# Cross attention of a decoder layer: scores of a late and an early tile made together, in four rows of 32x32 tiles

## The chip, the core and the metric

The kernel runs on one NeuronCore of a Trainium2 chip. The metric is the device time of one execution in microseconds (us). A core has engines that run side by side, each with its own queue of instructions in program order: TensorE (PE in the rows; its weight loads are PEld), VectorE (DVE), ScalarE (ACT), GpSimd (POOL) and SyncE (SP), which issues the transfers here. They wait for each other by semaphores. TensorE writes into PSUM, 8 banks of 128 partitions by 512 fp32 columns.

## What is computed

One post-norm decoder layer over 128 sequences of 64 tokens, 128 features, all in fp32: linear attention with 16 heads, a feed-forward layer with a table lookup, cross attention, and a small mixture of experts. The change touches the cross attention and the last lines of the mixture's gate. Cut to them:

```python
def _L0_xattn_ref(x, encoder_output, mask, WQ, WK, WV, WO):      # H = 16 heads of 8
    q = (x @ WQ)...; k = (encoder_output @ WK)...; v = (encoder_output @ WV)...
    scores = jnp.einsum('bhqd,bhkd->bhqk', q, k) / SQRT_DK
    future = jnp.triu(jnp.ones((s, s), jnp.int32), 1)
    m = mask[:, None, :, None] + future[None, None, :, :]
    scores = jnp.where(m != 0, NEG, scores)
    attn = jax.nn.softmax(scores, axis=-1)
    ctx = jnp.einsum('bhqk,bhkd->bqhd', attn, v).reshape(b, s, d)
    return ctx @ WO
```

The gate is a softmax over 7 experts, of which the two largest weights are kept, divided by their sum, and used on one expert's output.

## The kernel before

The 8192 tokens are 64 tiles of 128, in 16 groups of four. Three phases run over the groups one after the other: linear attention (phase 1), feed-forward (phase 2) and, from about 250 us on, cross attention and mixture (`phase3` of each engine, called with step s). In step s of phase 3 the attention of group s is done, the projections of group s+1 are prepared, the attention output of group s-1 is projected, added and normalised and its experts are multiplied, and the mixture of group s-2 is finished. Each step has four slots, t = 0 to 3, one for each tile n = 4s + t. The order of the work is written out by hand: each engine's `phase3` lists, slot by slot, what it does, and runs it in that order.

**Late and early tiles.** A tile holds 32 queries of four sequences. An even n is a late tile (queries 32 to 63, over all 64 keys), an odd n an early one (queries 0 to 31, over the 32 keys that they may see). Late scores take all 512 columns of the two banks of `pair[0]`, early scores 256 columns of the two banks of `pair[1]`.

**Scores.** TensorE's array is used in 32x32 tiles. A quad is four heads: 32 rows of features of `qT` (so one row of tiles of the array), and a matmul of quad and sequence gives 32 queries by 4 heads of keys. `k_exp` holds the keys of each of the four heads apart, zero elsewhere, so that one matmul gives all four. `scores_open(n)` writes the causal mask as the start of the sum (L1228, bf16, 8 matmuls in rows 0 and 2 of the array) and adds quads 0 and 2 (L1210, 8 matmuls, each of which runs as two passes and so has two records); `scores_close(n)` adds quads 1 and 3 (L1210). Quads 0 and 1 go into one bank, 2 and 3 into the other, so the two of one bank are in different calls.

**From scores to output.** DVE `shift(n)` takes the largest score of each head (L930) and subtracts it (L936 early; L943 late, in two halves); ACT `probabilities(n)` takes the exponential (L718); PE `turn_probabilities` transposes it back into the score banks (L1242), late 8 transposes, early 4; ACT `copy_pT` copies it out (L725); PE `weigh_values` multiplies by the values into bank 7 (L1270 late, L1254 and L1261 early); DVE `xattend` divides (L918, L920). Since the turned probabilities use the score banks, `scores_open(n+2)` waits for `copy_pT(n)`.

**The rest of a step.** PE: `turn_y` (L1051, X), K and Q projections (L1279), V projection (L1290), attention transposes (L1342) and output projection (L1325), transposes of the normalised rows (L1051, xn), experts (L1298). DVE: residual add (L1011) and statistics (L290, L297) in slot 1, `gate_top` (L952 to L957) and `future_keys` (L1000) in slot 0, `gate_weights` (seven operations, each waiting for the one before, L972 to L982) in slot 2, `mixture` (L988 and statistics) in slot 3. POOL: `spread_k` (L514, makes `k_exp`), bias (L537), normalisation of group s-1 (L305 to L327, into `y2`), `spread_v` (L526), normalisation of group s-2 (the same lines).

## Time and profile before

| | |
|---|---|
| Median of 3 runs | 574.67 us (572.77, 574.67 and one of 655.31) |
| The profiled execution | 573.05 us, its span 571.3 us |
| TensorE busy | 514.6 us, 90% of the span |
| VectorE busy | 425.5 us, 74% |
| ScalarE busy | 358.6 us, 63% |
| GpSimd busy | 347.7 us, 61% |
| Chain that ended last | TensorE 74%, ScalarE 9%, VectorE 7%, issue 7% |

Busy shares are averages over the phases. In the rows a time like 399.08 is microseconds from the start of the span; the second number of a timeline row is how long its instructions were busy; the next row of the same engine can begin before that has passed, since instructions of an engine overlap, so the distance from start to start is what one costs its engine. What stands in square brackets is idle time just before, and who ended it.

### The profile page before, as it was taken

The numbers are of one execution on the slowest core, as the hardware profiler recorded it, in microseconds if no ns is written. First come the engines' busy times: TensorE is split into PE (matmuls) and PEld (weight loads), VectorE is DVE, ScalarE is ACT, GpSimd is POOL, SyncE is SP. The second block draws the span as 40 slices with busy tenths as digits, with TensorE's granted clock in tenths as the row PEclk, the third lists the DMA queues.
The fourth block names the chain that finished last, engine by engine and source line by source line (L and its number), as shares of the span: only waits on it lengthen the run. The fifth ranks groups of instructions, "written<-read, shape, count | busy, mean of one in ns | idle before, by whom it ended". The sixth has DMA issues, their size and how long they took to land.

```text
span 571.3 us, 23478 instructions
## 1 busy us (share of the span) xinstructions
PE 514.6 (90%) x9568; PEld 371.0 (65%) x9568; DVE 425.5 (74%) x1468; ACT 358.6 (63%) x643; POOL 347.7 (61%) x666
## 2 busy tenths in 40 slices
PE   2899999989999999988999999999999999999740
PEld 1677777767777777665666666666666666666530
DVE  2777777656777666565778898889888898889743
ACT  1565656657777778748657765677657666677320
POOL 6666666644577766631556666765776657765463
PEclk9999999999999999999999999999999999999775
DMA  6630000000000000011001011110111011100001
GB/s 165 178 100 2 3 2 3 2 3 1 1 2 1 2 1 2 1 40 27 26 3 48 5 49 50 49 27 26 49 50 47 7 49 49 50 22 3 23 18 37
DMA packets 24731, 17.47 MB, mean 31 GB/s; under 512 B 2096, under 2 KB 22448, under 8 KB 24624
## 3 DMA queue, kind: packets, MB, share of 16 engines
q1 hardware_dynamic: 24192, 15.90, 9.8%
q8 instruction: 76, 1.25, 0.9%
q14 instruction: 31, 0.25, 0.2%
q10 hardware_dynamic: 432, 0.07, 0.1%
HBM read 11.77 MB, written 4.19 MB: 28 GB/s over the span
## 4 chain that ended last, share of the span: by engine, by line
PE 74%; ACT 9%; DVE 7%; issue 7%; POOL 3%; DMA 1%; DVEq 0%; POOLq 0%; ACTq 0%
PE pair L1196 10%; PE pair L1160 9%; PE pair L1056 8%; PE pair L1242 7%; PE pair L1210 6%; PE pair L1051 6%; PE pair L1279 4%; PE pair L1270 3%; PE pair L1128 3%; ACT v L706 3%; PE pair L1298 3%; PE pair L1290 2%; PE pair L1228 2%; PE pair L1325 2%; ACT gel L718 2%
## 5 line engine op out<-in xcount | busy, mean ns | idle before, releaser
L725 ACT ACTIVATE gel<-pair 128x1024 f32<-128x1024 f32 x64 | 51.9, 810 | 63.0 <-PE pair L1242 63.0
L718 ACT ACTIVATE gel<-gel,row_scale 128x512 f32<-128x512 f32 x96 | 66.1, 720 | 33.1 <-DVE gel L943 20.7
L1210 PE MATMUL pair<-k_exp,qT 32*32 32x128 f32 (+1 forms) x2048 | 68.5, 327 | 0.2 <-PE pair L1210 0.2
L1196 PEld LDWEIGHTS pair<-w,gel 128*128 128x128 f32 x512 | 60.4, 192 | 8.0 <-issue 5.7
L1196 PE MATMUL pair<-w,gel 128*128 128x128 f32 x512 | 62.5, 276 | 1.0 <-ACT gel L651 1.0
L930 DVE TENSOR_REDUCE neg_max<-pair 128x16 f32<-128x1024 f32 x64 | 60.8, 950 | 1.6 <-PE pair L1210 1.3
L1160 PE MATMUL pair<-hT,w 128*128 128x512 f32 x128 | 58.2, 595 | 1.3 <-ACT lev L646 1.3
L1242 PE MATMUL pair<-ident,gel 128*128 128x128 f32 x384 | 56.1, 282 | 2.4 <-ACT gel L718 2.4
L526 POOL COPY v<-v 32x256 f32<-32x256 f32 x64 | 26.6, 416 | 51.3 <-ACT v L706 48.3
L1242 PEld LDWEIGHTS pair<-ident,gel 128*128 128x128 f32 x384 | 42.2, 141 | 21.1 <-issue 15.3
L514 POOL TENSOR_SCALAR k_exp<-k_sb,quad_mask 128x512 f32<-128x512 f32 x64 | 43.0, 687 | 6.0 <-issue 3.6
L1051 PE MATMUL pair<-ident,xn 128*128 128x128 f32 x192 | 31.5, 289 | 16.1 <-POOL xn L327 16.1
L1298 PE MATMUL pair<-w_moe,y2T 128*128 128x263 f32 x128 | 39.7, 440 | 6.7 <-ACT moe_out L732 6.0
L305 POOL TENSOR_SCALAR veps_b<-mv_b 128x4 f32<-128x4 f32 x32 | 7.7, 242 | 62.4 <-DVE mv_b L297 32.0
L943 DVE TENSOR_TENSOR gel<-pair,neg_max 128x512 f32<-128x512 f32 x64 | 41.2, 686 | 1.1
L491 POOL TENSOR_TENSOR X<-X,proj_sb 128x512 f32<-128x512 f32 x16 | 20.3, 1272 | 35.6 <-ACT proj_sb L609 35.6
L1051 PEld LDWEIGHTS pair<-ident,xn 128*128 128x128 f32 x192 | 23.4, 147 | 28.1 <-issue 17.0
L1160 PEld LDWEIGHTS pair<-hT,w 128*128 128x128 f32 x128 | 22.9, 190 | 23.8 <-issue 23.5
L651 ACT ACTIVATE gel<-lev 128x512 f32<-128x512 int8 x64 | 36.3, 619 | 0.1
L307 POOL TENSOR_TENSOR rstd_b<-veps_b,minus_half 128x4 f32<-128x4 f32 x32 | 34.1, 1065 | 2.7
L290 DVE BATCH_NORM_STATS2 stats<-X 128x6 f32<-128x128 f32 x128 | 27.6, 278 | 10.2 <-DMA X<-in_x 10.2
L307 POOL TENSOR_TENSOR rstd<-veps,minus_half 128x4 f32<-128x4 f32 x32 | 33.2, 1038 | 2.7
(127 smaller groups left out, 1231.4 us busy)
## 6 DMA issues: line engine op xcount, KB each, us to landing
X<-in_x SPq DMA_DIRECT2D x16, 256.0 KB, 3.0
cT<-in_ctx SPq DMA_DIRECT2D x16, 256.0 KB, 3.8
out_rows<-X SPq DMA_DIRECT2D x16, 256.0 KB, 2.5
mask_rows<-in_mask_early SPq DMA_DIRECT2D x16, 128.0 KB, 3.8
w<-in_L_attn_w SPq DMA_DIRECT2D x2, 256.0 KB, 3.4
w_kv<-in_L_attn_wk SPq DMA_DIRECT2D x1, 64.0 KB, 3.0
w_q<-in_L_attn_wq ACTq DMA_DIRECT2D x1, 64.0 KB, 2.6
w_kv<-in_L_attn_wv SPq DMA_DIRECT2D x1, 64.0 KB, 2.9
```

The source lines that it names most:

```text
L307: nc.gpsimd.tensor_tensor(rstd[:, :], veps[:, :], minus_half[:, :], ALU.pow)\
L514: last = nc.gpsimd.tensor_scalar(k_exp[q][:, h, :], k_sb[:, :], quad_mask[:, h:h + 1], 0.0, ALU.mult, ALU.add)
L718: nc.scalar.activation(part, part, ACT.Exp, scale=row_scale[:, n:n + 1])\
L725: nc.scalar.activation(pT[par], flat[:, 0:GW] if n % 2 else flat, ACT.Copy)\
L930: nc.vector.tensor_reduce(neg_max[par][:, :].rearrange("p (a h) -> p a h", a=2), scores, AX.X, ALU.max, negate=True).then_inc(max_ready, 1)
L1051: last = nc.tensor.transpose(dst[:, P * t:P * (t + 1)], src[:, t, :], ident[:, :])
L1056: last = nc.tensor.matmul(dst[:, P * t:P * (t + 1)], src[:, P * t:P * (t + 1)], w, start=True, stop=True)
L1160: nc.tensor.matmul(bank(up_bank(s, f)), w_1[:, P * f:P * (f + 1)], hT[p][:, :], start=True, stop=True).then_inc(up_done, 1)
L1196: last = nc.tensor.matmul(bank(6 + q)[:, P * t:P * (t + 1)], gel[:, q, f, P * t:P * (t + 1)], w_2[:, f, :], start=(f == 0), stop=(f == NF ...
L1210: last = nc.tensor.matmul(pair[t % 2][b * QW:(b + 1) * QW, quad // 2, heads], qT[p][rows, batch + first:batch + first + QW], k_exp[p][rows ...
L1242: last = nc.tensor.transpose(flat[:, P * i:P * (i + 1)], probability_rows(n)[:, P * i:P * (i + 1)], ident[:, :])
L1298: nc.tensor.matmul(bank(MOE_BANK[t])[:, 0:2 * D + NE], y2T[:, P * t:P * (t + 1)], w_moe[:, :], start=True, stop=True).then_inc(moe_done, 1)
```

## The change

TensorE makes the scores of late tile n+2 and early tile n+3 in one `scores_open` and one `scores_close`, both in the even slots. The late tile opens with quads 0 and 2 and the early one with quads 1 and 3; they close the other way round. So each call has all four rows of the array, going to four different banks. The early tile's mask is written from rows 1 and 3; for that the mask's constants are filled for all four blocks of 32 partitions (four selects of 32 partitions in place of two of 64, in phase 2 on POOL). The early tile's turned probabilities go into columns 256 to 511 of their banks, so its next scores need not wait for their copy, but for its `shift` (`sub_ready`). VectorE's `shift` of an even tile waits until both closes are done, and of an odd one also for the copy of the early probabilities before, since both use one bank.

The order in `phase3` is written anew on PE, DVE and ACT. POOL's and SP's is as before. `gate_weights` takes six operations in place of seven: `top_sum` is the product of the sum and its reciprocal.

```diff
@@ ACT @@
-                flat = pair[par][:, :, :].rearrange("p a c -> p (a c)")
-                nc.scalar.activation(pT[par], flat[:, 0:GW] if n % 2 else flat, ACT.Copy)\
+                turned = pair[par][:, :, HH * QW:] if n % 2 else pair[par][:, :, :]
+                nc.scalar.activation(pT[par].rearrange("p (a c) -> p a c", a=2), turned, ACT.Copy)\
                     .then_inc(pT_ready, 1)
...
@@ DVE @@
             def shift(n, par):
 
-                dve.wait_ge(s_done, n + 1)
+                dve.wait_ge(s_done, n + 2 if n > 0 and n % 2 == 0 else n + 1)
+                if n % 2:
+                    after(dve, pT_ready, n - 1)
...
-                chain(nc.vector.tensor_tensor(top_w[:, :, :], top_p[:, :, :],
-                                              top_s[:, :].unsqueeze(2).broadcast_to([P, TG, 2]),
-                                              ALU.mult))
-                chain(nc.vector.tensor_reduce(top_sum[:, :], top_w[:, :, :], AX.X, ALU.add))
+                chain(nc.vector.tensor_tensor(top_sum[:, :], top_z[:, :], top_s[:, :], ALU.mult))
...
@@ PE @@
+            def scores_open(*ns):
+
+                n = ns[0]
+                after(pe, pT_ready, n - 1)
+                if n > 1:
+                    pe.wait_ge(sub_ready, shifted(n - 1, 0))
+                if n % TG == 0:
+                    pe.wait_ge(kexp_ready, n // TG + 1)
+                    pe.wait_ge(q_ready, n // TG + 1)
+                for n in ns:
+                    future_scores(n)
+                for n in ns:
+                    quad_scores(n, (1, 3) if n % 2 else (0, 2)).then_inc(s_opened, 1)
+
+            def scores_close(*ns):
+
+                pe.wait_ge(s_opened, ns[-1] + 1)
+                for n in ns:
+                    quad_scores(n, (0, 2) if n % 2 else (1, 3)).then_inc(s_done, 1)
...
+                    if exists(s) and t % 2 == 0 and n + 2 < NT:
+                        scores_open(n + 2, n + 3)
                     if exists(s):
                         if t == 0:
                             pe.wait_ge(v2_ready, s + 1)
-                        if s == 0 and t == 0:
+                        if n == 0:
                             pe.wait_ge(ysum_ready, NG)
-                        if s * TG + t + 2 < NT:
-                            scores_open(s * TG + t + 2)
-                        weigh_values(s * TG + t, t, p)
+                        weigh_values(n, t, p)
+                    if exists(s) and t % 2 == 0 and n + 2 < NT:
+                        scores_close(n + 2, n + 3)
```

On TensorE, slots 2 and 3 of a step in the middle of phase 3 stand before like this (`k_exp,qT` are quads, `causal_bf` the mask, `ident,gel` the turned probabilities, `v,gel` the weighing, `ident,xn` the transposes into bank 6):

```order
L1242 MATMUL pair<-ident,gel 128x128 x8
L1290 MATMUL pair<-w_xv,cT 64x64 x16
L1228 MATMUL pair<-causal_bf,ident_bf 32x512 x8
L1210 MATMUL pair<-k_exp,qT 32x256 x8
L1270 MATMUL pair<-v,gel 32x18 x32
L1210 MATMUL pair<-k_exp,qT 32x256 x8
L1242 MATMUL pair<-ident,gel 128x128 x4
L1051 MATMUL pair<-ident,xn 128x128 x4
L1228 MATMUL pair<-causal_bf,ident_bf 32x256 x8
L1210 MATMUL pair<-k_exp,qT 32x128 x8
L1254 MATMUL pair<-v,future 32x144 x4
L1261 MATMUL pair<-v,gel 32x36 x16
```

The same slots of the changed kernel:

```order
L1267 MATMUL pair<-ident,gel 128x128 x8
L1315 MATMUL pair<-w_xv,cT 64x64 x16
L1236 MATMUL pair<-causal_bf,ident_bf 32x512 x8
L1236 MATMUL pair<-causal_bf,ident_bf 32x256 x8
L1221 MATMUL pair<-k_exp,qT 32x256 x8
L1221 MATMUL pair<-k_exp,qT 32x128 x8
L1295 MATMUL pair<-v,gel 32x18 x32
L1221 MATMUL pair<-k_exp,qT 32x256 x8
L1221 MATMUL pair<-k_exp,qT 32x128 x8
L1267 MATMUL pair<-ident,gel 128x128 x4
L1062 MATMUL pair<-ident,xn 128x128 x4
L1279 MATMUL pair<-v,future 32x144 x4
```

The early tile's mask and quads have moved out of slot 3 and stand directly behind the late tile's in slot 2; slot 3 has no scores left.

On VectorE, from the `xattend` of slot 1 to the start of `gate_weights`, with the semaphores waited for, before:

```order
L918 RECIPROCAL rec<-pair 128x16 [waits pv_done]
L920 TENSOR_TENSOR att<-pair,rec 128x128 [waits xrec_ready]
L930 TENSOR_REDUCE neg_max<-pair 128x16 [waits s_done]
L936 TENSOR_TENSOR gel<-pair,neg_max 128x512 [waits p_xposed,max_ready]
L972 TENSOR_REDUCE top_z<-top_e 128x4 [waits tope_ready]
```

The same stretch of the changed kernel:

```order
L931 TENSOR_REDUCE neg_max<-pair 128x16 [waits pT_ready,s_done]
L937 TENSOR_TENSOR gel<-pair,neg_max 128x512 [waits p_xposed,max_ready]
L917 RECIPROCAL rec<-pair 128x16 [waits pv_done]
L919 TENSOR_TENSOR att<-pair,rec 128x128 [waits xrec_ready]
L973 TENSOR_REDUCE top_z<-top_e 128x4 [waits tope_ready]
```

The early `shift` now stands ahead of the `xattend` of slot 1. In the whole step VectorE's order is now: `gate_top`, `future_keys`, `xattend` (slot 0); late `shift`, residual add and statistics, early `shift`, `xattend`, `gate_weights` (slot 1); `xattend` (slot 2); late `shift`, `xattend`, early `shift`, `mixture` (slot 3). Before, each slot began with one `shift`, and `xattend` ended it.

## Rows read from the trace of the kernel before

**Rows 1.** Windows: busy time by engine, granted clock, DMA share; phase 2, a light, a full step
```profile
150.00:200.00 50.00, 50.00 (x291) 36.61 (x291) 35.35 (x153) 37.31 (x73) 36.17 (x74) 1.00 0.01 1
...
269.00:287.20 18.20, 17.65 (x459) 12.25 (x457) 12.11 (x33) 12.23 (x21) 7.49 (x15) 1.00 0.09 26
397.25:415.51 18.26, 17.71 (x459) 12.18 (x458) 16.25 (x55) 12.39 (x22) 12.10 (x23) 1.00 0.14 39
```

**Rows 2.** Timeline, TensorE, one full step: start, busy, line, operands, count
```profile
391.56 0.66 PE L1051 MATMUL pair<-ident,xn 128*128 128x128 f32 x4
...
395.83 0.71 PE L1298 MATMUL pair<-w_moe,y2T 128*128 128x263 f32 x2 [0.44 <-ACT moe_out L732]
...
399.08 0.41 PE L1228 MATMUL pair<-causal_bf,ident_bf 32*32 32x512 bf16 x8
399.31 0.61 PE L1210 MATMUL pair<-k_exp,qT 32*32 32x256 f32 x16
399.85 0.74 PE L1270 MATMUL pair<-v,gel 128*32 128x18 f32 x64
400.52 0.66 PE L1210 MATMUL pair<-k_exp,qT 32*32 32x256 f32 x16
401.12 0.66 PE L1242 MATMUL pair<-ident,gel 128*128 128x128 f32 x4
...
403.45 0.30 PE L1228 MATMUL pair<-causal_bf,ident_bf 32*32 32x256 bf16 x8
403.57 0.40 PE L1210 MATMUL pair<-k_exp,qT 32*32 32x128 f32 x16
403.90 0.45 PE L1254 MATMUL pair<-v,future 128*32 128x144 f32 x8
...
404.59 0.45 PE L1210 MATMUL pair<-k_exp,qT 32*32 32x128 f32 x16
404.96 1.09 PE L1242 MATMUL pair<-ident,gel 128*128 128x128 f32 x8
```

**Rows 3.** Timeline, VectorE, the same step
```profile
399.08 0.36 DVE L952 MAX8 top<-moe_out 128x8 f32<-128x8 f32 x4
...
400.72 0.26 DVE L918 RECIPROCAL rec<-pair 128x16 f32<-128x16 f32 x1 [0.57 <-PE pair L1270]
...
401.29 1.22 DVE L930 TENSOR_REDUCE neg_max<-pair 128x16 f32<-128x1024 f32 x1
402.55 1.29 DVE L943 TENSOR_TENSOR gel<-pair,neg_max 128x512 f32<-128x512 f32 x2
403.76 0.68 DVE L1011 TENSOR_TENSOR X<-X,pair 128x512 f32<-128x512 f32 x1
...
406.03 0.22 DVE L918 RECIPROCAL rec<-pair 128x16 f32<-128x16 f32 x1
...
406.50 0.68 DVE L930 TENSOR_REDUCE neg_max<-pair 128x16 f32<-128x512 f32 x1
...
407.82 0.18 DVE L972 TENSOR_REDUCE top_z<-top_e 128x4 f32<-128x32 f32 x1
...
409.12 0.16 DVE L982 TENSOR_REDUCE top_sum<-top_w 128x4 f32<-128x8 f32 x1
409.31 0.26 DVE L918 RECIPROCAL rec<-pair 128x16 f32<-128x16 f32 x1
...
412.27 1.69 DVE L988 SCALAR_TENSOR_TENSOR moe_out<-moe_out,top_sum 128x128 f32<-128x128 f32 x4
...
415.55 0.23 DVE L918 RECIPROCAL rec<-pair 128x16 f32<-128x16 f32 x1
```

**Rows 4.** Timeline, POOL, a later full step
```profile
507.78 0.23 POOL L305 TENSOR_SCALAR veps_c<-mv_c 128x4 f32<-128x4 f32 x1 [1.15 <-DVE mv_c L297]
...
511.33 2.69 POOL L514 TENSOR_SCALAR k_exp<-k_sb,quad_mask 128x512 f32<-128x512 f32 x4
513.99 1.29 POOL L537 TENSOR_TENSOR moe_out<-moe_out,bias_bc 128x512 f32<-128x512 f32 x1
516.63 0.24 POOL L305 TENSOR_SCALAR veps_b<-mv_b 128x4 f32<-128x4 f32 x1 [1.35 <-issue]
```

More of the change, by code:

```diff
@@ L443, in late_constants @@
                 if part in (1, 2):
-                    b = part - 1
-                    c = causal[b * S:(b + 1) * S, :, :]
-                    const(select(out=c, in_=c, compare_op=ALU.is_ge, fill=NEG, base=S - QW,
-                                 pattern=[[0, HH], [-1, S]], channel_multiplier=1))
+                    for b in (2 * part - 2, 2 * part - 1):
+                        c = causal[b * QW:(b + 1) * QW, :, :]
+                        const(select(out=c, in_=c, compare_op=ALU.is_ge, fill=NEG, base=S - QW,
+                                     pattern=[[0, HH], [-1, S]], channel_multiplier=1))
                 if part in (3, 4):
@@ L754, in phase3 @@
                         nc.scalar.activation(attT[:, :], bank(6), ACT.Copy).then_inc(xattT_ready, 1)
+                    if t == 0 and exists(nxt):
+                        copy_y(nxt)
                     if t == TG - 1 and exists(prev):
@@ L1006, in phase3 @@
                 for t in slots:
-                    if exists(s) if t < TG - 1 else exists(s + 1):
-                        shift(s * TG + t + 1, (t + 1) % 2)
+                    n = s * TG + t
+                    if n == 0:
+                        shift(1, 1)
+                    if t == 0 and exists(old):
+                        dve.wait_ge(moe_ready, (s - 1) * TG)
+                        gate_top(old, p)
+                    if t == 0 and exists(s + 1):
+                        future_keys(s + 1, q)
+                    if t == 0 and exists(s):
+                        after(dve, xatt_xposed, s - 1)
+                        xattend(n, p, t)
+                    if t == 1 and exists(s):
+                        shift(n + 1, 0)
                     if t == 1 and exists(prev):
@@ L1016, in phase3 @@
                                       stats_b, mv_b, ln_b.done, prev)
+                    if t == 1 and exists(s):
+                        shift(n + 2, 1)
+                        xattend(n, p, t)
+                    if t == 1 and exists(old):
+                        gate_weights(old)
+                    if t == 2 and exists(s):
+                        xattend(n, p, t)
+                    if t == 3 and exists(s + 1):
+                        shift(n + 1, 0)
+                    if t == 3 and exists(s):
+                        xattend(n, p, t)
+                    if t == 3 and exists(s + 1) and s >= 0:
+                        shift(n + 2, 1)
                     if t == 3 and exists(old):
                         mixture(old, p)
-                    if t == 0 and exists(old):
-                        dve.wait_ge(moe_ready, (s - 1) * TG)
-                        gate_top(old, p)
-                    if t == 0 and exists(s + 1):
-                        future_keys(s + 1, q)
-                    if t == 2 and exists(old):
-                        gate_weights(old)
-                    if exists(s):
-                        if t == 0:
-                            after(dve, xatt_xposed, s - 1)
-                        xattend(s * TG + t, p, t)
             pipeline(dve, phase1, last=NG - 1)
@@ L1213, in quad_scores, with future_scores @@
                             k_exp[p][rows, :, batch:batch + width],
-                            start=False, stop=quad % 2 == 1)
+                            start=False, stop=quad % 2 != n % 2)
                 return last
-            def scores_open(n):
-                after(pe, pT_ready, n - 1)
-                if n % TG == 0:
-                    pe.wait_ge(kexp_ready, n // TG + 1)
-                    pe.wait_ge(q_ready, n // TG + 1)
+            def future_scores(n):
                 width = QW if n % 2 else S
                 for half in range(2):
-                    rows = slice(half * FH, half * FH + QW)
+                    quad = 2 * half + n % 2
+                    rows = slice(quad * QW, (quad + 1) * QW)
                     future = causal_bf[rows, :].rearrange("p (h k) -> p h k", k=S)[:, :, S - width:]
@@ L1344, in phase3 @@
                         last.then_inc(xatt_xposed, 1)
+                    if t == 0 and exists(g):
+                        after(pe, moe_ready, (s - 1) * TG - 1)
+                        after(pe, v2_ready, g)
+                        turn_y(g)
+                    if t == 1 and exists(r):
+                        pe.wait_ge(xattT_ready, r + 1)
+                        rows_product(bank(6), attT, w_xo[:, :]).then_inc(xproj_done, 1)
                     if t == 1 and exists(g):
@@ L1347, in phase3 @@
                         project_qk(yT, w_xq, bank(4), xq_done)
+                    if t == 2 and exists(g):
+                        pe.wait_ge(q_ready, g + 1)
+                        project_v(g, q)
+                    if t == 3 and exists(r):
+                        pe.wait_ge(ln_b.done, r + 1)
+                        transposes(y2, bank(6), y2_xposed)
+                    if exists(s) and t % 2 == 0 and n + 2 < NT:
+                        scores_open(n + 2, n + 3)
                     if exists(s):
```

82 lines of the change are left out of this document (30 added, 52 removed).

## The prediction

> **What bounds the kernel now.** I read the windows first, then the timelines of the engines over one step. The change touches phase 3 only, so the question is what sets the length of one step there. In the windows [rows 1] a full step takes 18.26 us, with TensorE busy for 17.71 and VectorE for 16.25; the granted clock is 1.00, the higher of the two levels (2.4 GHz). A light step, of the first two, has no mixture yet: 18.20 us, TensorE 17.65, VectorE only 12.11. So TensorE sets the light steps. In a full step TensorE's timeline shows one wait, 0.44 us ahead of the expert matmul that needs its bank copied out [rows 2]: 18.26 - 0.44 = 17.82 us of work. VectorE's busy sum leaves out what lies between dependent operations on itself; its timeline has one real wait, 0.57 us for the weighing in slot 0 [rows 3], so its own work takes 18.26 - 0.57 = 17.69 us. Two engines are full within 0.6 us of each other. Whatever TensorE saves in a full step, VectorE gives back only up to 0.57 us of it. That is the core of this forecast.
>
> **What the change saves on TensorE.** From start to start [rows 2]: the late tile's mask and quads 0 and 2 take 399.85 - 399.08 = 0.77 us (0.23 and 0.54), its closing quads 401.12 - 400.52 = 0.60. The early tile's take 403.90 - 403.45 = 0.45 (0.12 and 0.33) and 404.96 - 404.59 = 0.37. A pair costs 2.19 us. If the early tile's matmuls run in the two rows of the array that the late tile leaves free, a pair costs what the late tile costs, 1.37 us, and up to 0.05 more for the starts of another 24 matmuls. Do they run together? Before, two rows by four columns do: 8 matmuls of 256 columns in 0.54 us and of 128 columns in 0.33, so the time goes with the columns of one and hardly with the count. Four rows by four columns are not in the trace. Bounds: from below 1.37, nothing added; from above 2.19 for rows that do not overlap. I take 1.42, because the weighing, a 128-row form that reads all four row blocks at once for four column tiles, starts 64 passes in 400.52 - 399.85 = 0.67 us, about 10 ns each, and nothing there is slower for using all rows. TensorE saves 2 x (2.19 - 1.42) = 1.5 us a step: 17.82 becomes 16.3.
>
> The Trainium skill, TensorEngine Tiling (Array Packing), Instruction Overhead, puts some 60 cycles of overhead on each matmul. By it the 80 starts of a pair (16 masks, 64 passes of quads) would cost about 2.0 us at 2.4 GHz, an estimate from that page, whether they share the array or not, and the change would save next to nothing. The trace disagrees: passes start 10 ns apart in the weighing.
>
> **What VectorE has left.** The gate loses one operation; from the last one's start to the next instruction is 409.31 - 409.12 = 0.19 us [rows 3]. I take 0.2. Its work becomes 17.49 us. All its other operations are only reordered. So a full step can't be shorter than 17.49, and the question is what waits the new order leaves.
>
> Pieces from start to start [rows 3]: `gate_top` and `future_keys` 400.72 - 0.57 - 399.08 = 1.07; `xattend` 406.50 - 406.03 = 0.47 (0.5 below); late `shift` 403.76 - 401.29 = 2.47; add and statistics 406.03 - 403.76 = 2.27; early `shift` 407.82 - 406.50 = 1.32; gate 409.31 - 407.82 - 0.2 = 1.29; mixture 415.55 - 412.27 = 3.28. A signal from one engine to another takes about 0.13 us behind the end shown (weighing ends at 399.85 + 0.74 = 400.59, VectorE starts at 400.72).
>
> Wait one: slot 2. `scores_open(n+2, n+3)` waits for the early `shift` just done. Then TensorE needs 0.13 + 0.79 (open) + 0.67 (weigh) + 0.63 (close) + 0.13 = 2.35 us until the late `shift` may start. VectorE meanwhile does `xattend`, gate, `xattend`: 0.5 + 1.29 + 0.5 = 2.29. It waits 0.1 us. In slot 0 the same loop is covered by mixture, `gate_top` and `future_keys`, over 4.3 us.
>
> Wait two: slot 3. K is now projected at the end of slot 0 and copied in slot 1, so POOL's `spread_k` starts later, and POOL's pieces close up into one chain behind the mixture's statistics [rows 4]: normalise group s-2 511.33 - 507.78 = 3.55, spread 2.66, bias 1.29, normalise group s-1 3.45 (the same operations as the 3.55), 10.9 us. With 0.3 for the signal ahead (their wait of 1.15 ended that long after the statistics), then 0.13, transposes 0.66, weighing 404.59 - 403.90 = 0.69, 0.13, the `xattend` of slot 3 is free 12.8 us after the mixture. VectorE gets there after 1.07 + 0.5 + 2.47 + 2.27 + 1.32 + 0.5 + 1.29 + 0.5 + 2.47 = 12.4. It waits 0.4, or 0.3 if it has already waited 0.1. TensorE's wait for the same transposes, near 0.8 us, falls into its 1.2 us of slack.
>
> The added waits of the early `shift` (copy of the probabilities before) and of the late one (both closes) cost nothing: the copy lies some 3 us earlier, behind the turn in slot 1, and the early close ends with the late one. Without that cover a `shift` would hold up everything behind it on VectorE. The expert matmul's 0.44 us wait on TensorE goes too, since the turn now stands ahead of it. The two extra selects on POOL lie in phase 2, where TensorE is busy for 50.00 of 50 us and POOL for 36 [rows 1]; nothing.
>
> **The sum.** Full step: 17.49 + 0.1 + 0.3 = 17.9 us against 18.26, 0.35 saved; some twelve of them, 4.2. Light steps: the one in the rows, and the next, whose mixture comes only at its end, so that VectorE goes through it with the room of the one before. TensorE 18.20 - 1.5 = 16.7, 1.5 saved each, 3.0. The first fill, the last two steps and the emptying, where engines wait for each other in a chain, I leave as they are. 573.05 - 7.2 = 565.9, say **566 us**, against a profiled execution of 573.05; that lies within 2 us of the two close runs of before (572.77 and 574.67).
>
> The page's rule on the PSUM Bottleneck (TensorEngine Tiling (Array Packing), the Trainium skill) says that tiling speeds up TensorE but not the reading of PSUM. The trace agrees: 0.57 us of room on VectorE against 1.5 saved.
>
> **Rivals.**
> - *The waits don't appear.* If POOL's chain or the loop in slot 2 is 0.4 us shorter than I make it, a full step falls to 17.49: 12 x 0.77 + 3.0 = 12.2, 560.8 us. For it: both waits are small differences of long sums. Against it: both sums are on the edge at once. 16%.
> - *Scores overlap in part.* With 0.15 us more in both open and close, wait one becomes 0.4, and the full steps save 0.1 to 0.2: 1.8, the light ones 1.8: 569.5. With the waits a bit longer, up to 573. 14%.
> - *The other side: the four rows don't overlap.* A pair costs 2.19 as before, open 1.22 and close 0.97. Then in slot 2 TensorE needs 0.13 + 1.22 + 0.67 + 0.97 + 0.13 = 3.12 us against VectorE's 2.29: it waits 0.83, and a full step takes 17.49 + 0.83 + 0.3 = 18.6: 12 x 0.36 = 4.3 us lost, 577 us. It decides from about 0.3 us more in each call. For it: the form is not in the trace. Against it: two rows do overlap, into two banks, and here are four banks. 7%.
> - *Starts bind, as by the page.* Then 2.0 us a pair, near 576. 2%.
> - *A wait that I don't see* holds VectorE for 1 us a step (the V copy, moved to slot 2, or the early order of the copies on ScalarE, 12.4 us busy of 18.3): 585. 3%.
>
> The forecast itself, 563 to 569.5, has the other 58%.
>
> **The numbers.** From 560 to 573 holds the forecast, nearly all of the first rival and the second. About 2%, 11.5 us, is what a measurement of this kernel can tell from no change: faster than 561.5 is two thirds of the first rival and a little of the forecast's edge, 14%; slower than 584.5, 3%; the rest within.
>
> **What would show it.** Right: in the changed profile a close of late and early quads takes about 0.6 us from start to start, and an open 0.8; the full step is 17.9 us, with VectorE idle for 0.1 us for the quads and 0.3 for the early weighing and TensorE idle for 1.2 us or more, ahead of the masks (for the early `shift`) and of the `xn` transposes (for POOL); POOL without a pause from L305 of group s-2 to L327 of group s-1. Wrong: quads of 0.9 us, a step above 18.2, or VectorE waiting for a semaphore of ScalarE.

## The result, and the profile after

| | before | changed |
|---|---|---|
| Median | 572.7 us (20 runs) | 575.63 us (20 runs, from 571.04) |
| Ratio to before | 1 | 1.0043, 95% interval 1.0027 to 1.0059 |
| Profiled execution, its span | 573.05, 571.3 us | 575.97, 574.2 us |
| TensorE busy | 514.6 us, 90% | 498.4 us, 87% |
| VectorE busy | 425.5 us, 74% | 415.1 us, 72% |

The change takes 16 us of busy time off TensorE and 10 off VectorE, and the kernel is 0.4% slower: its interval lies above 1, though well inside the 2% that the prediction counts as no change. 566 was forecast, with a range from 560 to 573. One run of each kernel, of 655.31 and of 2618.49 us, stands far above its others and hardly moves a median of 20.

First the timeline of TensorE over one step of the changed kernel in which little is disturbed (one stop of 0.20 us, at 410.78; start, busy, line, operands, count; idle time before in brackets). It answers to [rows 2].

```profile
399.86 0.60 PE L1062 MATMUL pair<-ident,X 128*128 128x128 f32 x4
400.39 0.41 PE L1236 MATMUL pair<-causal_bf,ident_bf 32*32 32x512 bf16 x16
400.61 0.70 PE L1221 MATMUL pair<-k_exp,qT 32*32 32x256 f32 x32
401.24 0.78 PE L1295 MATMUL pair<-v,gel 128*32 128x18 f32 x64
401.95 0.66 PE L1221 MATMUL pair<-k_exp,qT 32*32 32x256 f32 x32
402.54 1.13 PE L1304 MATMUL pair<-cT,w_xk 128*128 128x512 f32 x2
...
409.11 0.41 PE L1236 MATMUL pair<-causal_bf,ident_bf 32*32 32x512 bf16 x16 [0.47 <-ACT gel L724]
...
412.50 0.66 PE L1062 MATMUL pair<-ident,xn 128*128 128x128 f32 x4 [0.18 <-POOL xn L326]
...
417.03 0.60 PE L1062 MATMUL pair<-ident,X 128*128 128x128 f32 x4
```

An open takes 401.24 - 400.39 = 0.85 us and a close 0.59: a pair 1.44. The step takes 17.17 us against 18.26. So the saving is there. But most steps don't look like this. In TensorE's waits from 250 to 545 us (line, what was waited for, us in total, times, longest) the changed kernel has these two entries:

```profile
PE pair L1221 <- issue: 10.7, 9, 2.1
PE pair L1295 <- issue: 2.1, 3, 1.3
```

In the kernel before, the same view has these:

```profile
PE pair L1261 <- issue: 0.6, 1, 0.6
PE pair L1270 <- issue: 0.5, 1, 0.5
```

"Issue" is time in which an engine waited for nothing that the profile shows. Here is one such place, on TensorE's timeline:

```profile
463.06 0.71 PE L1221 MATMUL pair<-k_exp,qT 32*32 32x256 f32 x32
463.70 0.77 PE L1295 MATMUL pair<-v,gel 128*32 128x18 f32 x64
464.40 0.61 PE L1221 MATMUL pair<-k_exp,qT 32*32 32x256 f32 x2
467.09 1.10 PE L1221 MATMUL pair<-k_exp,qT 32*32 32x256 f32 x30 [2.08 <-issue]
```

Two passes of a closing quad run, then the engine stands still for 2.1 us in the middle of one call, which has no wait inside it, and then the other 30 run. VectorE waits for these quads. Its busiest groups on the page answer for that: first of the changed kernel,

```profile
L931 DVE TENSOR_REDUCE neg_max<-pair 128x16 f32<-128x1024 f32 x64 | 60.6, 946 | 16.2 <-PE pair L1221 15.6
```

where before the idle time ahead of that operation was 1.6 us.

**Where the time went.** TensorE's transposes of X mark the steps of phase 3. Before:

```profile
251.95 0.60 PE L1051 MATMUL pair<-ident,X 128*128 128x128 f32 x4
268.89 0.60 PE L1051 MATMUL pair<-ident,X 128*128 128x128 f32 x4
287.09 0.60 PE L1051 MATMUL pair<-ident,X 128*128 128x128 f32 x4
507.59 0.60 PE L1051 MATMUL pair<-ident,X 128*128 128x128 f32 x4
```

and changed:

```profile
253.11 0.60 PE L1062 MATMUL pair<-ident,X 128*128 128x128 f32 x4
271.02 0.60 PE L1062 MATMUL pair<-ident,X 128*128 128x128 f32 x4
292.84 0.60 PE L1062 MATMUL pair<-ident,X 128*128 128x128 f32 x4
508.83 0.60 PE L1062 MATMUL pair<-ident,X 128*128 128x128 f32 x4
```

The last row is twelve steps behind the third. From the differences of these rows, with the kernel of the experiment e4 (below; its four rows start at 253.06, 271.21, 288.65 and 500.65, its span is 562.4) beside them:

| us | before | changed | forecast of the difference | difference | e4, difference to before |
|---|---|---|---|---|---|
| up to the first | 251.95 | 253.11 | 0 | +1.2 | +1.1 |
| two light steps | 35.14 | 39.73 | -3.0 | +4.6 | +0.5 |
| twelve full steps | 220.50 | 215.99 | -4.2 | -4.5 | -8.5 |
| the rest | 63.7 | 65.4 | 0 | +1.7 | -2.0 |
| span | 571.3 | 574.2 | -7.2 | +2.9 | -8.9 |

The full steps come out as forecast, but by two errors that cancel, as will be seen; the rest of the miss lies in the light steps and at the ends.

### The profile page after: what moved, and what is told of

Same layout as the page of the kernel before. It is cut to its first block, busy times and chain, and to the rows that moved or that the text cites. A ratio compares the mean times of both kernels' runs of the same rounds, so it can differ in the third digit from the quotient of the medians.

```text
span 574.2 us, 23512 instructions
## 1 busy us (share of the span) xinstructions
PE 498.4 (87%) x9568; PEld 376.2 (66%) x9568; DVE 415.1 (72%) x1452; ACT 356.5 (62%) x643; POOL 346.8 (60%) x668
## 3 DMA queue, kind: packets, MB, share of 16 engines
q8 instruction: 76, 1.25, 0.9%
## 4 chain that ended last, share of the span: by engine, by line
PE 69%; DVE 12%; POOL 7%; issue 7%; ACT 2%; DMA 1%; DVEq 0%; POOLq 0%; ACTq 0%
PE pair L1067 9%; PE pair L1207 9%; PE pair L1171 9%; PE pair L1221 6%; PE pair L1062 6%; PE pair L1267 5%; PE pair L1323 5%; PE pair L1304 4%; DVE neg_max L931 3%; PE pair L1139 3%; PE pair L1295 3%; POOL k_exp L513 2%; DVE gel L944 2%; PE pair L1081 2%; PE pair L1097 2%
## 5 line engine op out<-in xcount | busy, mean ns | idle before, releaser
L1221 PE MATMUL pair<-k_exp,qT 32*32 32x128 f32 (+1 forms) x2048 | 49.4, 332 | 10.8 <-issue 10.7
L1267 PEld LDWEIGHTS pair<-ident,gel 128*128 128x128 f32 x384 | 44.1, 143 | 21.0 <-issue 15.3
L304 POOL TENSOR_SCALAR veps_c<-mv_c 128x4 f32<-128x4 f32 x16 | 3.9, 246 | 84.1 <-DVE mv_c L296 73.2
L1062 PE MATMUL pair<-ident,xn 128*128 128x128 f32 x192 | 32.1, 294 | 19.6 <-POOL xn L326 19.4
L1221 PEld LDWEIGHTS pair<-k_exp,qT 32*32 32x32 f32 x2048 | 26.1, 103 | 16.7 <-issue 13.5
```

Source lines behind the costliest of these rows:

```text
L1062: last = nc.tensor.transpose(dst[:, P * t:P * (t + 1)], src[:, t, :], ident[:, :])
L1221: last = nc.tensor.matmul(pair[t % 2][b * QW:(b + 1) * QW, quad // 2, heads], qT[p][rows, batch + first:batch + first + QW], k_exp[p][rows ...
L1267: last = nc.tensor.transpose(dst, probability_rows(n)[:, P * i:P * (i + 1)], ident[:, :])
```

## The theory

**Supply.** All long "issue" gaps inside a group of like matmuls fall at one place of TensorE's instruction count. With all of its records in the trace (weight loads, matmul passes and its semaphore instructions) numbered by their start, from 0, the first record behind such a gap has the remainder 193 on division by 256, in every kernel of this study. That record is called the border of a block below. TensorE's instructions come in by transfers of their own: on the page the queue

```profile
q8 instruction: 76, 1.25, 0.9%
```

moves 76 packets of 1.25 MB in all, 16 KB each, and TensorE has 19489 records, 76.1 times 256. In e4, with 18721 records (73.1 times 256), it moves 73 packets. So instructions arrive in blocks of 256. The theory: when TensorE uses up a block faster than the next can be had, it stands still at the border. A block of the new dense stretch (open, weighing, close: some 290 records in 2.2 us, where before it was some 200 with slower work on both sides) is used up in as little as 1.8 us. From the records, time to use up a block, from 252 to 545 us. A gap is given here, and in the table of the experiments, from the start of the record before it to the start of the one behind: 2.45 us for the stop of 2.08 above.

| | before | changed |
|---|---|---|
| blocks used up in under 2.9 us; followed by a gap over 0.3 us; gaps | 1; 0; none | 8; 8; 0.9 to 2.5 us |
| in 2.9 to 4 us | 18; 2; up to 0.8 | 13; 4; up to 1.4 |
| in over 4 us | 37; 1; 0.4 | 35; 0; none |

The gaps at borders inside masks, quads and weighing sum to 2.0 us in 3 places before, and 16.7 in 12 after; of that, TensorE is idle for 1.1 and 12.8 us. The number of instructions is not the reason: a full step has 924 records before and 925 after. The new order only sets them closer.

**The transfers themselves.** The trace has the time of each of the 76 packets, and they settle the theory. Four stops of the changed kernel, in us:

| TensorE begins a block | packet of the next block starts | has landed | TensorE begins the next block | after landing |
|---|---|---|---|---|
| 282.04 | 283.80 | 284.68 | 286.09 | 1.41 |
| 417.57 | 417.56 | 418.91 | 420.31 | 1.40 |
| 461.81 | 464.64 | 465.59 | 467.09 | 1.50 |
| 519.29 | 520.40 | 521.65 | 523.10 | 1.45 |

All 12 gaps of the changed kernel end 1.2 to 1.5 us after a packet has landed, the two over 0.5 us of the kernel before 1.4 us after, and those of e3 (below) 1.2 to 1.6. In none of the traces of this study does any block begin sooner than 1.19 us after its packet has landed. So a packet's transfer starts about when TensorE begins the block before it (in the changed kernel from 0.9 us ahead to 2.8 behind, 1.1 behind in the median), takes about 1.0 us, and its instructions can run some 1.4 us later. An estimate from these three: a block that is used up in less than their sum, 3.5 us in the usual case, ends in a stop. The sum varies; in the 12 gaps it was from 2.7 to 5.3 us.

**The stops cost a second time, by the clock.** The granted clock of TensorE falls to the lower of its two levels (1.2 GHz) behind three of the longer stops of the changed kernel (1.85, 2.08 and 1.62 us), at about 286, 467 and 525 us. Windows around the second (busy time of PE, PEld, DVE, ACT, POOL, then the granted clock), and TensorE's timeline there:

```profile
463.00:467.00 4.00, 2.01 (x114) 1.26 (x99) 1.72 (x9) 1.65 (x3) 3.70 (x8) 1.00 0.21 52
467.00:471.00 4.00, 3.91 (x79) 2.69 (x78) 2.51 (x3) 1.47 (x3) 0.83 (x2) 0.57 0.01 4
```

```profile
468.12 1.11 PE L1267 MATMUL pair<-ident,gel 128*128 128x128 f32 x4
469.03 1.06 PE L1062 MATMUL pair<-ident,xn 128*128 128x128 f32 x4
470.02 0.68 PE L1279 MATMUL pair<-v,future 128*32 128x144 f32 x8
```

The transposes of the normalised rows take 470.02 - 469.03 = 0.99 us from start to start, against 0.59 in the step shown first (412.50 to 413.09). The stretch from 467.09 to 470.94 costs TensorE some 1.4 us more than the same work there, so the three cost about 4 us, an estimate. In the kernel before, and in e4, the clock stays at 1.00 from 252 to 525 us. The second step of phase 3 shows both prices: 21.8 us against e4's 17.4, of which two stops are 0.92 + 1.85 and the clock some 1.4. Stops of 0.62 and 1.62 us and the third stretch lie behind 508.83, in "the rest" of the table above, which is 1.7 us longer than before.

The rival: the gaps are hidden semaphore waits, or the four rows of the array disturb each other, or the new order has a wait that the trace doesn't name.

## The experiments

All on the changed kernel except where a base is named. The ratio is to the kernel before, with its 95% interval. "Gaps" are those at block borders inside masks, quads or weighing over the whole kernel, from about 0.14 us up, in us (from start to start, as above) and places.

| | us | ratio | records per step | gaps |
|---|---|---|---|---|
| e1 same rows | 582.4 | 1.0186 (1.0129, 1.0243) | 925 | 12.3 in 11 |
| e2 border beside the dense stretch | 572.6 | 0.9993 (0.9972, 1.0014) | 1023 | 14.1 in 19 |
| e3 border in the dense stretch | 601.3 | 1.0494 (1.0453, 1.0535) | 1023 | 38.5 in 28 |
| e4 few masks | 566.0 | 0.9891 (0.9829, 0.9954) | 877 | 3.9 in 5 |
| e11 the same again | 567.4 | 0.9905 (0.9874, 0.9936) | 877 | 5.6 in 5 |
| e5 before, few masks | 578.6 | 1.0094 (1.0070, 1.0118) | 876 | 0.9 in 3 |
| e6 few masks, same rows | 574.9 | 1.0035 (1.0012, 1.0059) | 877 | 4.8 in 7 |
| e7 before, gate of six | 571.6 | 0.9977 (0.9965, 0.9990) | 924 | 1.9 in 4 |
| e8 borders moved once | 572.2 | 0.9972 (0.9940, 1.0005) | 925 | 8.5 in 9 |
| e9 slot 0 spread | 583.9 | 1.0197 (1.0179, 1.0216) | 925 | 14.4 in 12 |
| e10 few masks, slot 0 spread | 579.9 | 1.0125 (1.0094, 1.0157) | 877 | 5.8 in 7 |

**e2 and e3: moving the borders.** Tiny matmuls (32x32x32, bf16, two records each) fill a step up to four blocks, so that the borders stay at the same work in every step. The two kernels differ in one number: where e2, shown here, has `fillers(50, 5)` once ahead of the first step, e3 has `fillers(114, 5)`, 128 records more.

```diff
+            def fillers(count, dst):
+                for i in range(count):
+                    r = slice(i % QB * QW, (i % QB + 1) * QW)
+                    nc.tensor.matmul(bank(dst)[r, 0:32], ident_bf[r, r], causal_bf[r, 0:32],
+                                     start=True, stop=True)
...
                         scores_close(1)
+                        fillers(50, 5)
...
+                    if t == 2 and s > 0 and exists(g):
+                        pe.wait_ge(k_ready, g + 1)
+                        fillers(12, 5)
+                    if t == 3 and s > 0 and exists(g):
+                        fillers(37, 5)
```

> The changed kernel with small extra matmuls (2 instructions each, into a free bank, results unused): 12 in slot 2 and 37 in slot 3 of steps 1 to 14, where TensorE waits anyway, so that a step has about 1024 instructions, four blocks of 256; and 50 once ahead of the first step, so that a block's border falls in the middle of each dense stretch (open, weigh, close: 290 instructions in 2.1 us). Theory S: the gaps inside quads and weighing nearly vanish (under 2 us of 12.8) and the time is 562 to 568 us, though there is more to do. Theory R, or any theory in which the blocks don't matter: gaps as before, 575 us or a little more.

> The same as the kernel with the split blocks, but 114 extra matmuls ahead of the first step in place of 50, so that in every step a whole block lies inside a dense stretch. Theory S: a gap of 1 to 2.5 us at the end of nearly every dense stretch, some 28 of them, 30 to 50 us in all, of which each step's slack takes 1 to 2 us: 585 to 610 us. Theory R or no effect of blocks: the same time as the one with the split blocks plus the 0.6 us of the 64 further matmuls.

e3 is 28.7 us slower than e2, for 64 tiny matmuls once, of which 37 run in 0.36 us. TensorE's waits of e3:

```profile
PE pair L1221 <- issue: 26.9, 24, 1.9
```

and its timeline:

```profile
401.01 0.42 PE L1221 MATMUL pair<-k_exp,qT 32*32 32x128 f32 x8 [1.18 <-issue]
...
408.94 0.66 PE L1221 MATMUL pair<-k_exp,qT 32*32 32x256 f32 x24
410.73 0.42 PE L1221 MATMUL pair<-k_exp,qT 32*32 32x128 f32 x8 [1.13 <-issue]
411.08 1.76 PE L1304 MATMUL pair<-cT,w_xk 128*128 128x512 f32 x2
```

The stop is seven or eight passes before the end of a close, in slot 0 and slot 2 of step after step. No semaphore and no row of the array knows of this place; only the instruction count does. 27 blocks are used up in under 2.9 us, and 26 of them are followed by a gap over 0.3 us. e2 missed its expectation (562 to 568 us, gaps under 2): blocks that hold half of a dense stretch each are used up in 2.8 to 3.9 us, and most of these still end in gaps, mostly of 0.4 to 1 us, 14 us in all.

**e8: the borders moved once, no filling.** 64 tiny matmuls ahead of the first step.

```diff
                         scores_close(1)
+                        fillers(64, 5)
```

> The changed kernel with 64 tiny matmuls (128 instructions) once ahead of the first step of phase 3, nothing else: the borders of the 256-instruction blocks move by half a block against the work of every step, and a step still has 925 instructions. Supply theory: the gaps stay at the same place of TensorE's instruction count (remainder 193 of 256) but move to other lines and steps; since 925 instructions shift the border by 157 instructions in each step, the sum over sixteen steps stays about the same: 12 to 20 us of gaps, 572 to 579 us. The steps that were long (the second at 21.8 and the twelfth at 20.5 us) become ordinary and others become long. Rival (the long steps are waits of the schedule itself, in those steps): the same steps stay long.

The second and the twelfth step, 21.8 and 20.5 us long in the changed kernel, take 17.2 and 17.7; now the first (21.4) and the sixth (20.5) are long. The gaps of the table sum to 8.5 us; three more stand at borders outside that count (1.07 and 0.82 in projections and transposes, and one of 1.55 between a weighing and its close), 11.9 together, just under the 12 to 20 expected. The last of them is in the long first step:

```profile
258.91 1.11 PE L1221 MATMUL pair<-k_exp,qT 32*32 32x256 f32 x32 [1.34 <-issue]
```

There the granted clock is also at its lower level, from 255.6 to 262.4 us, behind a wait of 1.73 for VectorE that the changed kernel has too without losing the clock. So not all of that step is supply. But the second, sixth and twelfth step become ordinary or long as the count is moved, which rules out a wait of the schedule in those steps.

**e4, e5, e11: fewer instructions.** Four mask matmuls of 32x32 become one of 32x128, which writes the same bank.

```diff
-                    for b in range(QB):
-                        nc.tensor.matmul(pair[n % 2][b * QW:(b + 1) * QW, half, 0:HH * width],
-                                         ident_bf[rows, rows], future, start=True, stop=False)
+                    nc.tensor.matmul(pair[n % 2][:, half, 0:HH * width],
+                                     ident_rep[rows, :, :].rearrange("p b q -> p (b q)"),
+                                     future, start=True, stop=False)
```

> The changed kernel with the causal mask written by one matmul of 32 rows by 128 columns for each bank, in place of four of 32 by 32: 24 instructions fewer in each dense stretch (266 in place of 290), 48 fewer in a step. Theory S: the fraction of blocks that lie inside a dense stretch falls to near nothing but blocks of 2 to 3 us remain, so the gaps shrink by a third to a half: 569 to 574 us. Theory R: no change from the changed kernel, 575 us, or slower by the switches between tile forms (28 of 0.1 us).

> The kernel before, with only the few masks of e4_few_masks: each bank's mask written by one matmul of 32 rows by 128 columns in place of four of 32 by 32. It is the control for e4: how much of e4's gain has nothing to do with the pairing. A step has 877 instructions on TensorE here too. Supply theory (TensorE starves where a block of 256 instructions is used up in under about 3 us): before has few such gaps (1.96 us over phase 3), and the mask costs TensorE the same columns, so little is to be gained: 571 to 574 us, same as before. Rival (the few masks are a gain of their own, and e4 says nothing about the pairing): TensorE's share of a mask falls, 566 to 568 us.

> The kernel of e4_few_masks once more, in five rounds, for the interval: it had 565.99 us, ratio 1.1 per cent below before from four runs. Supply theory: 565 to 568 us again, ratio 0.987 to 0.992; clean steps 17.3 to 17.7 us. If its time depends on how the gaps fall from run to run, single runs spread over more than the 4 us of before.

The same edit makes the changed kernel 8 to 10 us faster and the kernel before 6 us slower. e5's timeline says why it costs something:

```profile
402.00 0.39 PE L1232 MATMUL pair<-causal_bf,ident_rep 32*128 32x512 bf16 x2
402.32 0.66 PE L1215 MATMUL pair<-k_exp,qT 32*32 32x256 f32 x16
402.91 0.74 PE L1275 MATMUL pair<-v,gel 128*32 128x18 f32 x64
```

Mask and quads take 0.91 us (0.32 and 0.59) where they took 0.77 (0.23 and 0.54) [rows 2]; the early tile's take 0.14 more too, and a step 18.55. Neither of the two cases given for e5 held: both had left out that the wide mask costs TensorE time. That makes the gain in e4 the clearer. It comes in spite of dearer masks, with the dense stretch 24 records shorter and the gaps down from 16.7 us to 3.9 and 5.6. e4 is faster than both kernels, and 3 us below its own expectation; no stretch of it between 252 and 525 us has the lower clock, which that expectation had not counted. That its 566.0 us is the figure forecast for the change is luck: other terms make it up, as shown below. e11 lands in its range; its single runs spread from 563.5 to 569.7 us, and its profiled one has the lower clock in one stretch, from 355 us.

**e1, e6: are four rows worth anything?** Both tiles' quads run in the same rows of the array again, in e1 on the changed kernel, in e6 on e4.

```diff
-                    quad = 2 * half + n % 2
-                    rows = slice(quad * QW, (quad + 1) * QW)
+                    rows = slice(half * FH, half * FH + QW)
-                    quad_scores(n, (1, 3) if n % 2 else (0, 2)).then_inc(s_opened, 1)
+                    quad_scores(n, (0, 2)).then_inc(s_opened, 1)
```

> The changed kernel, but the early tile's mask and quads use the same rows of the array as the late tile's in each call (mask and quads 0 and 2 open, 1 and 3 close), so the order is that of the changed kernel and the rows no longer overlap. Theory S (instruction supply: TensorE's instructions come in blocks of 256, and a block that is used up in under about 3 us leaves TensorE waiting for the next): a pair's open, weigh and close take about 2.9 us in place of 2.1, so the blocks last longer, the waits put down to issue inside quads and weighing fall from 12.8 us to under 5, but the loop in slot 2 costs VectorE 0.8 us a step; 575 to 579 us. Theory R (the four rows themselves disturb each other and make the gaps): no gaps, and the time falls below 572.

> e4_few_masks with the late and the early tile in the same rows of the array again (both open with quads 0 and 2): what the four rows are worth once most of the supply gaps are gone. The trace of e1 shows about 0.25 us more in an open and 0.2 in a close than the changed kernel. Supply theory with the prediction's own VectorE arithmetic: slot 2's loop grows by 0.45 us and VectorE waits that much longer once a step, light steps lose 0.9 each: 5 to 8 us more than e4, 571 to 574 us. Rival (the rows are worth nothing here, the order of the work alone gives the time): 566 to 568 us.

e1's timeline, an open, the weighing and a close:

```profile
402.22 0.52 PE L1235 MATMUL pair<-causal_bf,ident_bf 32*32 32x512 bf16 x16
402.56 0.83 PE L1221 MATMUL pair<-k_exp,qT 32*32 32x256 f32 x32
403.32 0.74 PE L1294 MATMUL pair<-v,gel 128*32 128x18 f32 x64
403.99 0.88 PE L1221 MATMUL pair<-k_exp,qT 32*32 32x256 f32 x32
404.80 1.12 PE L1303 MATMUL pair<-cT,w_xk 128*128 128x512 f32 x2
```

A pair takes 1.10 + 0.81 = 1.91 us against 1.44: four rows save 0.47 a pair, 0.94 a step. By the medians that is 6.8 us on the changed kernel and 8.9 on e4, where 5 to 8 were expected of e4. Of the 0.75 that a pair saves against before (2.19 to 1.44), 0.28 comes from issuing both tiles together and 0.47 from the rows. The forecast of few gaps for e1 was wrong: its dense stretch is only 0.4 us longer, and 12.3 us of gaps stay, so that its 582.4 us lies above the 575 to 579. With the rows apart and the gaps still there, the four rows aren't their cause.

**e7: the gate alone**, on the kernel before: six operations for seven.

> The kernel before with only the gate in six operations in place of seven. VectorE saves 0.19 us a step. The prediction took VectorE's own work for 17.69 of 18.26 us in before, TensorE sets the step with 17.82 of work plus its one wait of 0.44. Theory: the 0.19 lies on VectorE alone, and part of it reaches the step: 571 to 573 us (0 to 2 us faster). Rival (VectorE sets the full step already): the whole 0.19 in twelve to fourteen steps, 2.5 us faster, 570.3 us or less. Slower than 574 would speak against both.

1.3 us faster by the medians, with full steps of 18.27 as before. TensorE sets them, and VectorE's 0.2 us is not seen in them; where the 1.3 us comes from is not shown.

**e9, e10: spreading slot 0.** The transposes of attention output and X go between open and weighing, to thin out the dense stretch of slot 0 (in e10 on e4); shown for X, the other block moves with it.

```diff
-                    if t == 0 and exists(g):
-                        after(pe, moe_ready, (s - 1) * TG - 1)
-                        after(pe, v2_ready, g)
-                        turn_y(g)
...
                         scores_open(n + 2, n + 3)
...
+                    if t == 0 and exists(g):
+                        after(pe, moe_ready, (s - 1) * TG - 1)
+                        after(pe, v2_ready, g)
+                        turn_y(g)
                     if exists(s):
```

> The changed kernel with one change of order on TensorE: in slot 0 the transposes of the attention output and of X (eight matmuls, 32 instructions, 0.97 us) stand between the open and the weighing, not ahead of the open. Same instructions, same blocks. The dense stretch of slot 0 (about 290 instructions in 2.2 us) becomes 320 in 3.2 us, that of slot 2 stays. In the changed kernel's trace 4.7 us of the gaps lie in slot 0 and 12.1 in slot 2. VectorE weighs late in slot 0 by 0.97 us, behind the mixture's statistics, gate_top and future_keys, where e4's trace has some 0.85 us of room. Supply theory: the gaps of slot 0 vanish, those of slot 2 stay at about 12 us: 570 to 573 us. Rival (the order of slot 0 was right, and its gaps were filled by waits that come in their place): 575 to 578 us.

> e4_few_masks with the spreading of e9. e4 has only 0.7 us of gaps in slot 0, so by the supply theory little is left to win there: 564 to 567 us. If the later weighing of slot 0 is not covered (0.1 to 0.2 us a step), 567 to 569.

The gaps of slot 0 go as expected (4.7 us to 1.6, and in e10 to nothing), and the kernels are 8 and 12 to 14 us slower all the same. On TensorE's timeline of e10:

```profile
404.95 0.61 PE L1328 MATMUL pair<-w_moe,y2T 128*128 128x263 f32 x2
406.23 0.39 PE L1240 MATMUL pair<-causal_bf,ident_rep 32*128 32x512 bf16 x4 [0.67 <-ACT gel L725]
```

The transposes had covered ScalarE's copy of the turned probabilities, for which the open waits. Without that cover each step has this new wait: from 250 to 545 us the profile puts 17.8 us of waits of the masks down to that copy in 30 places in e9, against 7.5 in 15 in the changed kernel, and 18.4 in 30 in e10, against 8.5 in 16 in e4. In the row above the copy ends at 406.17, just before the masks. A gap was traded for a dearer wait. The rival's mechanism held, but its 575 to 578 us, and e10's 564 to 569, were too low.

## Why the prediction was wrong

- **Pair of tiles 1.42 us, four rows overlap: right.** 1.44; the bound of 1.37 from below was near, and e1 prices the rows at 0.47 a pair. The rival in which four rows don't overlap fell, and so did the one in which starts bind.
- **"Nothing there is slower for using all rows": the step that failed.** It priced a start at 10 ns from one group of 64 passes and took instructions to be always at hand. A price per start holds only while instructions arrive; the prediction had no term for their supply. The runs showed that supply is a term: the gaps at borders grew by 14.7 us (16.7 - 2.0; idle time alone by 11.7), and 3.5 us of them (1.3 and 2.2) lie in the second light step, with another 1.4 or so from the clock behind them. Not each microsecond of a gap reaches the end, since some fall where TensorE had slack: e4, with 11 to 13 us less of them, is 8 to 10 us faster. "A wait that I don't see" was the nearest rival, with 3%, and the places named for it were wrong.
- **VectorE's own work of 17.49 us: wrong by 0.5, the other way.** "All its other operations are only reordered" took their durations as fixed. The mixture's product (L988 before, L986 after) takes 469 ns on average in the full steps before and 343 after. Before, it starts at 412.27 [rows 3], and POOL's copy of V runs beside it:

```profile
412.43 1.87 POOL L526 COPY v<-v 32x256 f32<-32x256 f32 x4 [2.67 <-ACT v L706]
```

  In the changed kernel the same copy is over before the mixture starts; POOL's rows, then VectorE's:

```profile
412.39 1.83 POOL L525 COPY v<-v 32x256 f32<-32x256 f32 x4
...
419.38 0.25 POOL L304 TENSOR_SCALAR veps_c<-mv_c 128x4 f32<-128x4 f32 x1 [5.16 <-DVE mv_c L296]
```

```profile
416.28 1.13 DVE L986 SCALAR_TENSOR_TENSOR moe_out<-moe_out,top_sum 128x128 f32<-128x128 f32 x4
```

  Four products in 1.13 us in place of 1.69. By the Trainium skill, SBUF — State Buffer, Who interferes with whom, VectorE and GpSimd share a pair of ports, and a VectorE operation with two inputs in SBUF contends with a GpSimd one that reads SBUF. The trace agrees: 484 ns in the median where POOL mostly runs beside it, 341 to 352 where it doesn't. This gain, up to 12 x 4 x (0.469 - 0.343) = 6.0 us where VectorE sets the step, hid the loss in the full steps, where the sum came out right to 0.3 us for the wrong reasons. That is luck. e4 shows what they take with few gaps: 8.5 us saved, twice the forecast.
- **Light steps, 1.5 saved each: wrong.** The row taken for both was the second's. Even e4, with almost no gaps there, needs 35.6 us for the two, where 32.1 was forecast. In the first one ScalarE still does phase 2's last normalisations, and the copies for which the opens wait stand behind them; and the early `shift`, a wait that the change adds, is itself late there. ScalarE of the changed kernel, then TensorE's waits in that step:

```profile
261.62 1.64 ACT L335 ACTIVATE X<-X,offs_b,rstd_b 128x128 f32<-128x128 f32 x4
263.16 1.00 ACT L724 ACTIVATE gel<-pair 128x1024 f32<-128x1024 f32 x1
```

```profile
255.44 0.41 PE L1236 MATMUL pair<-causal_bf,ident_bf 32*32 32x512 bf16 x16 [1.73 <-DVE gel L937]
...
264.22 0.41 PE L1236 MATMUL pair<-causal_bf,ident_bf 32*32 32x512 bf16 x16 [1.19 <-ACT gel L724]
...
268.29 0.45 PE L1279 MATMUL pair<-v,future 128*32 128x144 f32 x8 [1.26 <-ACT gel L724]
```

  4.2 us of waits in one step, against 1.8 in three rows of the same step before. Whether another order of ScalarE would free them wasn't tried; this reading rests on the trace alone.
- **Wait one (slot 2, 0.1 us) and wait two (slot 3, 0.3 us): wrong, the first too small and the second too large.** VectorE in slot 2 of the step shown first:

```profile
411.26 0.26 DVE L917 RECIPROCAL rec<-pair 128x16 f32<-128x16 f32 x1 [0.65 <-PE pair L1295]
...
412.00 1.23 DVE L931 TENSOR_REDUCE neg_max<-pair 128x16 f32<-128x1024 f32 x1 [0.16 <-PE pair L1221]
```

  It is idle for 0.81 us in that loop. From the end of the early `shift` (409.01) to the late one it takes 2.99 us where 2.35 were summed; the gap at 410.78 makes the weighing 0.4 longer than the 0.71 of slot 0, and the rest lies in several small amounts. Wait two is not seen on VectorE there, though TensorE waits 0.18 for POOL's rows, whose chain runs without pause as foretold. e4, with few gaps, has these waits for weighing and quads at 5.7 + 5.3 us from 290 to 525 us, over 0.8 a step (its masks are dearer), where 0.4 was forecast. The expert matmul's wait of 0.44 is gone. Of the signs named for "right", quads of 0.6 and 0.85 us came true; TensorE idle for 1.2 us did not (0.47 + 0.20 + 0.18). The 0.47 is ahead of the masks, as foretold: the row names ScalarE's copy, but that ended at 408.63, and the early `shift` at 409.01, 0.10 before the masks start. Of those for "wrong", steps above 18.2 came true in five of fourteen, and VectorE waited for ScalarE once in the full steps (1.9 us).
- **The page against the trace.** The prediction weighed the rule of the Trainium skill, TensorEngine Tiling (Array Packing), Instruction Overhead, of some 60 cycles on each matmul, which is not borne out here either (64 passes in 0.7 us). The rule that bore on this case is in another page: the Trainium skill, Runtime: NRT & Kernel Launch, Instruction fetch mechanics, says that instructions come in blocks of 16 KiB, 256 of them, and that the fetch is hidden by an issue floor of some 20 cycles each. The first half agrees with the 76 packets and the 256-record spacing. The second does not: e3 uses up 27 blocks in 1.79 to 1.84 us, 7 ns a record, and behind 26 of them a gap of 0.4 to 2.2 us follows, in most over 1.2.

What stays open: why a packet's transfer starts now ahead of the border and now up to 2.8 us behind it. So no single duration tells whether a block is too fast: all eight of the changed kernel's blocks under 2.9 us had a gap, but two of e4's three had none, and from 2.9 to 4 us some have and some don't. How much of each stop and of each stretch of lower clock reaches the end is not measured singly. Why the first transposes of X start 1.2 us later wasn't followed up.

## What to carry to other kernels

Before packing small matmuls closer, count instructions and not only columns: where 256 records of TensorE (an fp32 matmul has four here: two loads, two passes; semaphore instructions count too) are to run in under about 3 us, put a stop of 1 to 2 us into the sum, and between 3 and 4 us a shorter one in some places. In a kernel packed like this one, a wide matmul in place of four narrow ones paid even at some cost in columns; in the kernel before it did not. When idle time is put down to "issue" in the middle of a group of like matmuls, number the records; gaps with one remainder on division by 256, each ending 1.2 to 1.6 us after a packet of the instruction queue has landed, are supply, and no reordering of semaphores cures them. Look at the granted clock behind a stop too. A reorder also changes durations: look at what ran beside each operation before and what will run beside it now, and take a first or last step of a pipeline from its own rows.

## What the runs showed of the hardware

TensorE can outrun its own instruction supply, with gaps of up to 2.5 us: no block of 256 begins sooner than 1.19 us after its 16 KB have landed, and they start to move about when the block before begins. Behind three of the longer stops of the changed kernel the granted clock fell to its lower level for some us. Moving a block border by 128 instructions moved this kernel by 29 us (e2 to e3) at nearly the same work. Two tiles' closing quads take 0.97 us in two calls before, 0.81 in one call in the same rows, and 0.59 in four rows. One 32x128 mask matmul costs 0.14 us more, with the quads behind it, than four of 32x32.
